# A graph and convolution layer on one core: slot rows by VectorE and memory, distances and gathers later in the group

## The reference

```python
h = maximum(layernorm(x), 0)
xc = h.T                                        # features x nodes
c = relu(bn(conv1d(xc, conv1_w)))               # 1 tap
c = bn(conv1d(c, conv2_w, pad=8))               # 17 taps
x_conv = relu(c + xc).T
s = h @ w_se.T + b_se                           # 3 numbers per node
dist = |s_n|^2 + |s_m|^2 - 2 s_n . s_m
A = exp(-dist) * adj
x_nmp = A @ relu(h @ w_msg.T + b_msg)
gi = concat(x_conv, x_nmp) @ w_ih.T + b_ih ; gh = h @ w_hh.T + b_hh
r = sigmoid(gi_r + gh_r) ; z = sigmoid(gi_z + gh_z) ; n = tanh(gi_n + r * gh_n)
out = x + (1 - z) * n + z * h
```

## Time and profile before

| | |
|---|---|
| median of 3 runs | 286.28 us (286.19 to 286.46) |
| the profiled execution | 286.3 us |
| its span | 284.4 us |
| TensorE matmul busy | 275.6 us, 97% of the span |
| VectorE busy | 241.5 us, 85% |
| ScalarE busy | 165.1 us, 58% |
| GpSimd busy | 63.8 us, 22% |
| granted TensorE clock | full speed in all 40 slices |
| one group of the steady part, start to start | 32.8 us |

### The profile page before, as it was taken

The page is one execution under the profiler, slowest core; times in us unless marked ns, Lnnn a source line. Parts: engine busy times, 40 slices in busy tenths (PEclk is TensorE's granted clock), DMA queues, the critical chain, the costliest instruction groups (busy, mean ns, idle before and its releaser), DMA issues.

```text
span 284.4 us, 5281 instructions
## 1 busy us (share of the span) xinstructions
PE 275.6 (97%) x1866; PEld 248.8 (87%) x1866; DVE 241.5 (85%) x544; ACT 165.1 (58%) x276; POOL 63.8 (22%) x125
## 2 busy tenths in 40 slices
PE   7899999999999999999999999999999999999993
PEld 6599877999888998899888998899888998899993
DVE  6998979988997989978998789968998787966565
ACT  3797468646656367546565367555674266571363
POOL 7600020820216002520116102430026100250000
PEclk9999999999999999999999999999999999999999
DMA  7820215555262604454252422655021540023002
GB/s 228 302 38 0 94 62 169 219 94 181 76 224 37 187 0 115 184 75 150 74 196 60 100 93 75 221 62 163 2 94 55 76 147 3 0 37 39 0 2 74
DMA packets 10429, 28.51 MB, mean 100 GB/s; under 512 B 2738, under 2 KB 4276, under 8 KB 9524
## 3 DMA queue, kind: packets, MB, share of 16 engines
q1 hardware_dynamic: 7712, 24.24, 24.0%
q0 software_dynamic: 2544, 3.93, 10.3%
q10 hardware_dynamic: 148, 0.01, 0.0%
HBM read 23.94 MB, written 7.91 MB: 112 GB/s over the span
## 4 chain that ended last, share of the span: by engine, by line
PE 68%; DVE 17%; issue 6%; ACT 5%; POOL 2%; DMA 1%; DVEq 0%; ACTq 0%; POOLq 0%
PE ps L1243 20%; PE ps L1245 19%; PE ps L1244 19%; PE ps L1327 4%; PE ps L1293 3%; DVE stats L787 2%; DVE wt_lo L829 2%; ACT wt_hi L462 1%; POOL rstd L383 1%; PE ps L1304 1%; DMA xin<-x_first 1%; DVE aff L985 1%; DVE v_lo L910 1%; DVE y L930 1%; PE ps L1317 1%
## 5 line engine op out<-in xcount | busy, mean ns | idle before, releaser
L1243 PE MATMUL ps<-v_hi,wt_hi 128*128 128x256 f32 x280 | 80.9, 289 | 0.4 <-DVE y L949 0.3
L1245 PE MATMUL ps<-v_hi,wt_lo 128*128 128x256 f32 x280 | 78.9, 282 | 0.0
L1244 PE MATMUL ps<-v_lo,wt_hi 128*128 128x256 f32 x280 | 78.6, 281 | 0.0
L1243 PEld LDWEIGHTS ps<-v_hi,wt_hi 128*128 128x128 f32 x280 | 52.8, 188 | 1.6 <-DVE y L949 0.5
L1244 PEld LDWEIGHTS ps<-v_lo,wt_hi 128*128 128x128 f32 x280 | 52.8, 188 | 0.3
L1245 PEld LDWEIGHTS ps<-v_hi,wt_lo 128*128 128x128 f32 x280 | 52.7, 188 | 0.0
L389 POOL TENSOR_TENSOR scale<-vpe,neg_half 128x8 f32<-128x8 f32 x6 | 10.6, 1767 | 87.9 <-DVE scale L804 87.9
L1243 PE MATMUL ps<-h_hi,wt_hi 128*128 128x512 f32 (+1 forms) x67 | 26.2, 391 | 0.2 <-ACT gate L643 0.2
L1245 PE MATMUL ps<-h_hi,wt_lo 128*128 128x512 f32 (+1 forms) x67 | 25.8, 386 | 0.0
L1244 PE MATMUL ps<-h_lo,wt_hi 128*128 128x512 f32 (+1 forms) x67 | 25.7, 384 | 0.0
L638 ACT ACTIVATE gate<-ps,par 128x512 f32<-128x512 f32 x14 | 9.6, 687 | 20.6 <-PE ps L1245 20.6
(11 more groups left out here) (166 smaller groups left out, 656.4 us busy)
## 6 DMA issues: line engine op xcount, KB each, us to landing
w<-ln_rows SPq DMA_DIRECT2D x6, 1024.0 KB, 4.8
mask<-adj_t SPq DMA_DIRECT2D x8, 512.0 KB, 3.5
out<-x_t SPq DMA_DIRECT2D x7, 512.0 KB, 5.2
out<-gate POOLq DMA_DIRECT2D x14, 256.0 KB, 4.0
xin<-x_nm SPq DMA_DIRECT2D x6, 512.0 KB, 3.2
xt<-x_t SPq DMA_DIRECT2D x6, 512.0 KB, 5.7
w<-w_conv SPq DMA_DIRECT2D x1, 576.0 KB, 6.5
gate<-w_gate SPq DMA_DIRECT2D x1, 576.0 KB, 7.5
```

The source lines that it names most:

```text
L1243: pe.matmul(dst, wt_hi[:, blk, :], hi, start=start, stop=False)
L1244: pe.matmul(dst, wt_hi[:, blk, :], lo, start=False, stop=False)
L1245: return pe.matmul(dst, wt_lo[:, blk, :], hi, start=False, stop=stop)
```

## The change

`BY_TRANSPOSE = 1`: groups 0 and 1 keep the old way. From group 2 on:

- The slots are turned by VectorE (`turn`, a block transpose of 128x256 into the new tile `turned`), stored by SyncE with four DMAs into a scratch tensor `slot_rows` in memory, and loaded from there by two DMAs into `rows` (`factor_loads`), the second shifted by 16 partitions. TensorE's four transposes and ScalarE's `factor_rows` go.
- `distance` stands behind `sub_conv` 6 instead of 1. Both gathers stand behind `sub_conv` 8 instead of 5 and 6.
- ScalarE's `exponent` stands behind the third `m_shared`, the `h_hi` and the `hg` copies of the next group; `xc_high` ahead of `ghn_rows` and both `n_high`. VectorE's masks stand behind the last `add_shared`, `n_low` behind `xc_low`.
- `conv1`'s second half goes to bank 1, which VectorE's joins read, instead of bank 7, and waits for the last join of the group. `messages` waits for both halves of conv1's rows from group 3 on.
- For half 0 `gates_xc` is issued ahead of `gates_n`, which now closes the sums.

```diff
+            def factor_loads(g):
+                done = g - 1 - BY_TRANSPOSE
+                sp.wait_ge(turned_ready, done + 1)
+                upto(sp, rows_landed, 32 * done)
+                for i in range(4):
+                    ns = slice(32 * i, 32 * i + 32)
+                    sp.dma_start(slot_rows.rearrange("(i s) q n -> s q i n", s=SLOT)[:, :, :, ns],
+                                 turned[ns].bitcast(F32).rearrange("s (q i) n -> s q i n", q=2)).then_inc(turned_stored, 16)
+                sp.wait_ge(turned_stored, 64 * (done + 1))
+                sp.wait_ge(dist_ps, g)
+                sp.dma_start(rows[:, 0:4:2, :].bitcast(F32), slot_rows).then_inc(rows_landed, 16)
+                sp.dma_start(rows[0:P - KD, 1:4:2, :].bitcast(F32), slot_rows[KD:P]).then_inc(rows_landed, 16)
...
             for g in range(1, NG):
+                if g > BY_TRANSPOSE:
+                    factor_loads(g)
                 if g + 2 < NG:
...
+            def turn(g):
+                done = g - 1 - BY_TRANSPOSE
+                dve.wait_ge(slots_ready, g + 1)
+                upto(dve, turned_stored, 64 * done)
+                dve.transpose(turned[:].bitcast(F32).rearrange("p b (k s) -> p b k s", k=2),
+                              slots[:, :, :, 0:KD].bitcast(F32).rearrange("p k b s -> p b k s")).then_inc(turned_ready, 1)
...
                 else:
+                    turn(g)
                     update(g - 1, 1)
...
+                elif dst == 1:
+                    pe.wait_ge(y_ready, 7 * g)
...
             def messages(g, first=0):
-                pe.wait_ge(c_ready, NCH * g + 1)
+                pe.wait_ge(c_ready, NCH * g + (NCH if g > BY_TRANSPOSE + 1 else 1))
...
             def distance(g):
-                pe.wait_ge(rows_ready, g + 1)
+                if g <= BY_TRANSPOSE:
+                    pe.wait_ge(rows_ready, g + 1)
+                else:
+                    pe.wait_ge(rows_landed, 32 * (g - BY_TRANSPOSE))
...
+            def n_last(g, c):
+                return c == 0 and g > BY_TRANSPOSE
...
+                if last:
+                    three(bank(4), IH(R, 1), *nm, False, True).then_inc(r_ps, 1)
+                    three(bank(5), IH(N, 1), *nm, False, True).then_inc(gin_ps, 1)
+                    three(bank(6), IH(Z, 1), *nm, False, True).then_inc(z_ps, 1)
+                    return
...
+                if n_last(g, c):
+                    three(bank(4), IH(R, 0), *xc, False, False)
+                    pe.wait_ge(n_lo_ready, NCH * g + 1)
+                    three(bank(5), IH(N, 0), *xc, True, False)
+                    three(bank(6), IH(Z, 0), *xc, False, False)
+                    return
```

More of the change, by code:

```diff
@@ L58, with gnn_kernel @@
 NPAR = 14
-def gnn_kernel(nc, x_first, x_nm, x_t, adj_t, w_in, w_conv, w_gate, par_in, row_in, bias_in, ln_rows, out):
+def gnn_kernel(nc, x_first, x_nm, x_t, adj_t, w_in, w_conv, w_gate, par_in, row_in, bias_in, ln_rows, slot_rows, out):
     ctx = ExitStack()
@@ L192, in gnn_kernel @@
             sem("zd_ready"), sem("out_ready"))
+        BY_TRANSPOSE = 1
         BY_MATMUL = 1
@@ L253, in distances @@
             engine.wait_ge(s_ready, 2 * g + 2)
-            upto(engine, rows_ps, g)
+            if g <= BY_TRANSPOSE + 1:
+                upto(engine, rows_ps, g)
+            else:
+                engine.wait_ge(turned_ready, g - 1 - BY_TRANSPOSE)
             left, right = slots[:, 0], slots[:, 1]
@@ L1522, in _ @@
                 sub_conv(g, 5)
-                gather(g, 0, 5)
+                if g <= BY_TRANSPOSE:
+                    gather(g, 0, 5)
                 sub_conv(g, 6)
-                gather(g, 1, 7)
+                if g <= BY_TRANSPOSE:
+                    gather(g, 1, 7)
+                else:
+                    distance(g)
                 sub_conv(g, 7)
                 sub_conv(g, 8)
+                if g > BY_TRANSPOSE:
+                    gather(g, 0, 5)
+                    gather(g, 1, 7)
                 gates_h(g, 0, ahead)
@@ L1530, in _ @@
                     conv1(g + 1, 0, 0)
-                    conv1(g + 1, 1, 7)
-                gates_n(g, 0)
-                gates_xc(g, 0)
+                    conv1(g + 1, 1, 7 if g <= BY_TRANSPOSE else 1)
+                if g <= BY_TRANSPOSE:
+                    gates_n(g, 0)
+                    gates_xc(g, 0)
+                else:
+                    gates_xc(g, 0)
+                    gates_n(g, 0)
                 if ahead:
```

99 lines of the change are left out of this document (63 added, 36 removed).

## The result

| | before | after |
|---|---|---|
| median | 286.28 us (286.19 to 286.46) | **283.76 us** (283.68 to 284.79) |
| ratio, 95% interval | | 0.992 (0.990 to 0.994) |
| profiled execution, span | 286.3, 284.4 us | 284.79, 283.0 us |
| VectorE busy | 241.5 us | 244.6 us |
| ScalarE busy | 165.1 us | 161.8 us |

The medians are of four executions each. Faster by 2.5 us, 0.7 above the forecast of 283.1 and inside its range. The four executions of the changed kernel are 283.68, 283.74, 283.79 and the profiled one, 284.79: one stands 1.0 above the rest. That is the first thing to explain, since the kernel before never strayed by more than 0.3.

The account below looks back on a forecast made before the run. TensorE's in-order issue was taken as the bound. Transposes -3.2, joined gather -0.5, group 2's wait +0.1 and last group +0.4 gave -3.2 us: 286.3 to 283.1 us, range 282.6 to 285.0.

Parts of the forecast that it names:

- The transposes, -3.2 us: TensorE's four slot transposes removed: 0.44 us in each of groups 3 to 7, 1.0 us in group 2 with its wait.
- The joined gather, -0.5 us: TensorE's two gather halves side by side: one of two 0.09 us operand changes saved in each of six groups.
- The forecast's lower bound: Least gain from putting the gather halves side by side: nothing, if the next stage pays the operand change twice.
- The masks' chain, wanted at T+14.7: VectorE and ScalarE up to the first mask product, seen T+14.5 (T: group 3's start on TensorE): fits by 0.2 us.
- The 0.1 us for group 2: TensorE's gather in group 2: slots come 0.8 us later, VectorE's second join some 0.3 late, a tie; 0.1 us loss.
- Behind the gather: Conv1's second half, `gates_xc` and bank 5 after the gather: their inputs come early, by 1.2 us at the least.
- rival 3: A ScalarE or VectorE queue behind the gather 0.5 us beyond its margin: 3 us lost, 286.1 us, no change; chance 0.05.
- The last group, +0.4 us: Last group without conv1 between gates: `n_lo` 0.2 us late at bank 5, Z's tanh 0.2 late with semaphores.
- The rows through memory: Turn, four stores (3 us), two loads (3 us): landing T+7.8, wanted T+11.3, 3.5 us early; T is group 3's start.
- signs of being right: Group starts 32.2 to 32.3 us apart, rows landing 3 us early without idle time, 0 to 0.1 us before the gather.
- the upper bound: Stores and loads of the rows at worst: four stores one after another (6.4) and two loads (9.6), 16 us.
- rival 2: Rows land late, each microsecond beyond T+11.3 (T: group start) paid six times; at 11 us path 291.5 us, slower; chance 0.10.

## Why the prediction came out

**The transposes, -3.2 us: right.** Measured -3.3 alone. Reading starts against the matmul count, with group 2 apart, gave it to 0.1 or 0.2.

**The joined gather, -0.5 us: wrong, it is 0.** The failed step is "The 0.09 us are the change of operands. Joined, one of the two changes goes". No change of operands costs anything to be seen: eight gather matmuls cost 8 x 0.112 = 0.90 us, joined or not, and the 0.81 us are the distance to a start that is noted early. The transposes, four matmuls of the same size, cost 0.44 by the same step. The forecast's lower bound, nothing, is what came (286.25 against 286.32), though not for its reason, that the next stage pays it twice. These 0.5 us are most of the 0.7 by which the forecast was too low.

**The masks' chain, wanted at T+14.7: right** to 0.1 us, and its margin of 0.2 too, as 0.65 us of delay costing 0.49 a group shows. The 0.1 us for group 2 is 0.15: 32.47 us against 32.32 in the others and 32.30 where the masks are wanted later. The 0.84 us that group 2 gained is 1.0 less this.

**Behind the gather: right.** No wait in the steady part, nothing of rival 3.

**The last group, +0.4 us: 0.5.** The Z tanh is 0.35 late where 0.2 was reckoned, the `n_lo` 0.2 as reckoned.

**The rows through memory: the mechanism right, the size wrong, and it was luck that it hardly showed.** I had them land at T+7.8, 3.5 us early; they land at T+10.1 in group 3 of the first profile, and after T+11.45 in group 2 or 5 of others. Of its signs of being right, "no idle time before the `rows` matmuls" and "the last `rows` load landing some 3 us before them" did not come. Both terms were too small: "3 us for the stores, overlapped but with 0.5 us each to issue" is 4.5, since one issue takes 0.61 to 0.66 and a store 3.2 to land, and "3 for the loads" is 3.9, since the second is issued 0.6 behind the first. Against the row of `scale`, 1.6 us, a store of four times the size lands in 2.0 when the DMA engines are free, and in 3.2 with `out` beside it. That `out` fills the engines just then I had in the earlier trace rows and used only as a reason for the upper bound; it should have gone into the sum. The Trainium skill (DMA: Bandwidth & Descriptors, Specifications) says that runs below 512 B are read, modified and written. No price of that can be picked out here: 32 KB in runs of 128 B take 0.4 us more to land than 8 KB in runs of 32 B. The traffic beside them costs three times that, 1.2 us.

So rival 2, with 0.10, is what most executions on another chip seem to show, at a smaller size: in the profiled one 2.1 us, in two groups of six, not 1.4 in each; the spans of the nine long ones are 1.4 to 3.8 us above the lowest. By that chip's median, 285.43, the change is worth 0.9 us. The forecast's number and sign hold by the first measurement; of its account of the rows only the sign of the margin holds, and that not in each group.

## What to carry to other kernels

A chain of DMAs that replaces an engine's work has a margin only after every issue, every landing and the traffic beside it are counted; where no row shows these, look at the whole spread of the executions and not at the median, since a late transfer shows in some of them only. What a queue shares with a transfer that nobody waits for (here the stores of `out`) is cheap to move away. A price for leaving a piece of work, read from starts, may be nothing but an early start of what comes next: hold the whole piece against its number of instructions, and run the joining alone.

## What the runs showed of the hardware that was not expected

- The issue of one of the six DMAs takes SyncE 0.57 to 0.66 us, where the store of `scale`, of 256 runs as well, takes 0.38. In groups 2, 5 and 6 single issues were stretched up to 1.5 us, most of them ending 0.24 to 0.42 us behind a packet of the instruction queue.
- Accumulating stores of GpSimd slow a store in another queue from 2.0 to 3.2 us. Spreading the issue over two queues makes each store slower (3.2 to 3.7) and gains nothing.
- VectorE's block transpose of 128x256 fp32 elements takes 0.45 us, as long as a subtraction of that size (0.42 for 264).
- Eight gather matmuls cost TensorE 0.90 us and sixteen 1.79, a step of 0.112 us each, also from one PSUM bank to the next; the start of the next kind of matmul is noted 0.03 us behind the last one's, and the step behind it is longer by the rest.
